# A depthwise convolution's running sum moved from SBUF into one PSUM bank, in strips of eight rows

## The chip, the cores and the metric

The kernel runs on one core of one Trainium2 chip. The metric is the device time of one execution in microseconds (us). A core has five engines that work side by side and meet at semaphores: TensorE (PE in the profile) for matmuls, VectorE (DVE), ScalarE (ACT), GpSimd (POOL) and SyncE (SP), which here only issues DMAs. SBUF is the working memory. PSUM is a smaller memory of eight banks of 512 float32 values per partition; TensorE writes its results there, and VectorE and ScalarE can read and write it.

## The reference, cut to what matters

The input x is 32 images of 56 x 56 pixels and 96 channels, float32. Two residual blocks follow each other: an outlook attention (values, logits from 2 x 2 means, softmax over nine neighbours, sum over overlapping windows, output projection), then a 3 x 3 convolution of each channel by itself. `_gn` is a group norm over three channels and all pixels of an image.

```
    x = x + _L0_conv_ref(_gn(x), L0_conv_W_v, L0_conv_W_a, L0_conv_b_a, L0_conv_W_o, L0_conv_b_o)
    x = x + _L1_conv_ref(_gn(x), L1_conv_w)
    return x
```

The second line is what the change touches. `_L1_conv_ref` clips its nine weights per channel and takes their sign, so the convolution is nine shifted copies of the normed image, each times a number per channel, added up.

## The kernel before, in words

Channels lie on 96 partitions and pixels along the free dimension. One pass of the loop, here called a body, handles one image in a fixed order written out by hand. It has 64 slots (`BODY`), numbered g, 32 for the upper and 32 for the lower half of the image (h is 0 or 1). In every slot TensorE spreads attention weights over channels into a PSUM tile `bc` (`broadcast`, L733), VectorE multiplies it by the values `VAL` into `prod` (`product`, L600), GpSimd adds the two halves of `prod` in 45 of the 64 slots (`pre_add`, L363), and TensorE multiplies by the output weights three slots later and accumulates in `acc` (`add_up`, L753). VectorE adds finished classes of pixels to `X1` (`add_class`, L611). `bc` has two buffers and `prod` four, so TensorE can run up to two slots ahead of VectorE.

Everything else is hung into these slots by the table `AT`: each engine runs through the slots in order and in each does what the table gives it. Entries of 64 and more belong to the next body's pass. The work of three images overlaps: the body of number i multiplies for image i, prepares image i+1 (transposes `IN`, group norm, logits `LOG`, values `V`, softmax), and convolves image i-1.

- Softmax: VectorE takes maxima, sums and inverses (L623, L627, L631); GpSimd subtracts, multiplies and forms the low part of a split number (`SUB` L345, `MUL` L351, `LOW` L356); ScalarE takes exponentials (`EXP` L464), scales the inverse (`UP` L467, in slot 42, which waits for the inverses of slot 43's VectorE work) and writes the high part (`HIGH` L475).
- The uses of the `side` banks: 44 times per body TensorE fills a PSUM bank (`fill_use`: value matmuls L692, logits L698, input transposes L704, output transposes L710, group-norm sums L721) and ScalarE reads it out (`read_use`: L426, L433, L440, L446, L451). The two banks `side[0]` and `side[1]` alternate: the fill of use n waits for the read of use n-2. Input transposes stand in slots 5, 7, 7, 8, 9, 10, 10; the first nine logits in 19 to 23 with up to three in one slot; output transposes in 55 to 60; values in 27 to 33 and 62 to 67. The first read of the values of a half waits until VectorE's last product of that half is done, since it overwrites `VAL`.
- The convolution: ScalarE copies `X1` to `ACC` (L498, slot 1) and, after the norm (`square_1` L506, then GpSimd's small steps L370 to L381), writes the normed image with a rim into `XP` (`rimmed` L527, slot 10). `centre_tap` (L534) starts the sum: ACC = a * ACC + b, in three parts of 19, 19 and 18 rows, in slots 12, 14 and 15. Then VectorE does 24 taps (`tap`, L647), eight taps times three parts: `scalar_tensor_tensor` reads the shifted rows of `XP`, multiplies by the sign, adds `ACC` and writes `ACC`. Both tensors lie in SBUF. They stand in slots 14 to 53. The output transposes wait for all of them.

Two shorter bodies run before the loop (no convolution yet) and one after it (convolution only).

Of the kernel before, what the change touches and what calls it, by code (L numbers as in the profile page):

```python
# [5 lines left out]
BATCH, SIDE, CH = 32, 56, 96  # L6
# [51 lines left out]

    V: ((27, 30, 33, 33), (62, 63, 65, 67)),
    LOG: ((19, 19, 21, 21, 21, 22, 22, 23, 23), (39, 39, 42, 43, 48, 48, 48, 51, 53)),  # L60
# [23 lines left out]
    "rimmed": 10,  # L84
    "centred": (12, 14, 15),
    "taps": (14, 17, 18, 18, 19, 20, 20, 21, 25, 29, 30, 31, 32, 34, 35, 45, 48, 48, 48, 50, 50, 52, 53, 53),
}
PRE = [g for g in range(BODY)
       if TERMS[2 * (g % SLOTS)][0] == TERMS[2 * (g % SLOTS) + 1][0] and g not in AT["not pre"]]
CUTS = (0, 19, 38, SIDE)  # L90
TAP_N = 3 * (KK - 1)
assert len(AT["taps"]) == TAP_N


def pieces(*kinds):
# [20 lines left out]
def upto(per_body, i, n):  # L116

    return (i + 1) * per_body + n


def build_program(nc, x, W_v, W_a, b_a, W_o, b_o, w_conv, ident, group, select, out):
# [3 lines left out]
    with ctx:  # L125
# [287 lines left out]
        def _(act):  # L413
            act.wait_ge(weights_in, 16 * N_W)

            def read_use(i, n, late, kind, which, k):
                bank = side[n % 2]
                until(act, side_full, upto(len(USES), i, n + 1))
                if kind == V:
                    h = which  # L420
                    r0, r1 = V_CUTS[h][k], V_CUTS[h][k + 1]
                    if k == 0:

                        until(act, prod_ready, upto(BODY, i - late, BODY if h else SLOTS))
                    top_row = 1 - h
                    ins = nc.scalar.activation(  # L426
                        VAL[h][:, top_row + r0:top_row + r1, 1:1 + SIDE],
                        bank[0:CH, 0:(r1 - r0) * SIDE].rearrange("c (r w) -> c r w", w=SIDE), ACT.Identity)
                elif kind == LOG:
                    h, cols = which, ROWS[which] * WIN  # L430

                    until(act, fine_step, done(FINE, i - 1, LOW, h, k))
                    ins = nc.scalar.activation(att[h][:, k, :], bank[0:QN, 0:cols],  # L433
                                               ACT.Identity, bias=ba[:, k:k + 1])
                elif kind == IN:
                    if k == 0:

                        until(act, x1_init, upto(1, i, 1))
                        until(act, pool_step, upto(4, i, 0))
                    ins = nc.scalar.activation(X0t[:, 4 * k:4 * k + 4, :],  # L440
                                               bank[0:CH, 0:4 * TP].rearrange("c (t p) -> c t p", t=4), ACT.Identity,
                                               accum_out=sums[:, 0, k:k + 1])
                elif kind == OUT:

                    act.wait_ge(y_out[k % 2], store_no(i, k))
                    ins = nc.scalar.activation(tok_out[:, k % 2, :, :],  # L446
                                               bank[0:TP, 0:4 * CH].rearrange("p (t c) -> p t c", t=4), ACT.Identity)
                else:
                    g = which
                    n_in = chunks(kind, g)  # L450
                    ins = nc.scalar.activation(spill[:, 0:n_in], bank[0:CH, 0:n_in], ACT.Identity,  # L451
                                               accum_out=(nmean if kind == GA else gvar)[:, g:g + 1])
                ins.then_inc(side_read, 1)
# [113 lines left out]
        def _(dve):  # L567
# [66 lines left out]
            def tap(i, n):  # L634
                t, part = divmod(n, 3)
                t += t >= KK // 2
                ty, tx = divmod(t, TAPS)
                r0, r1 = CUTS[part], CUTS[part + 1]
# [39 lines left out]
        def _(pe):  # L678
# [3 lines left out]
            def fill_use(i, n, late, kind, which, k):  # L682
                bank = side[n % 2]

                until(pe, side_read, upto(len(USES), i, n - 1))
                if kind == V:
                    h = which
                    r0, r1 = V_CUTS[h][k], V_CUTS[h][k + 1]
                    if k == 0:

                        until(pe, xn_ready, upto(2, i - late, h + 1))
                    last = nc.tensor.matmul(bank[0:CH, 0:(r1 - r0) * SIDE], wv[:, :], XN[:, r0:r1, :],  # L692
                                            start=True, stop=True)
                elif kind == LOG:
                    h = which
                    if k == 0:
                        until(pe, pool_normed, upto(2, i, h + 1))
                    last = nc.tensor.matmul(bank[0:QN, 0:ROWS[h] * WIN], wa[:, k, :, :],  # L698
                                            pooled[:, 0:ROWS[h], :], start=True, stop=True)
                elif kind == IN:  # L700
                    if k == 0:
                        until(pe, x_in, 16 * (i + 2))
                    for t in range(4):
                        last = nc.tensor.transpose(bank[0:CH, t * TP:(t + 1) * TP], tok_in[:, 4 * k + t, :], idn[:, :])  # L704
                elif kind == OUT:
# [3 lines left out]
                    for t in range(4):  # L709
                        last = nc.tensor.transpose(bank[0:TP, t * CH:(t + 1) * CH], ACCt[:, 4 * k + t, :],  # L710
                                                   idn[0:CH, 0:CH])
                else:
# [98 lines left out]
```

## Time and profile before

| | |
|---|---|
| three timed runs | 5112.86, 5118.91 (median), 5120.16 us |
| span of the profiled execution | 5120.9 us, 0.04% above that median |
| its time outside the span | the page gives none; the span is used as its own time |
| VectorE busy | 4730.3 us, 92% |
| TensorE busy | 4119.3 us, 80% |
| GpSimd busy | 4037.2 us, 79% |
| ScalarE busy | 2005.6 us, 39% |
| granted TensorE clock, mean | 0.850 of full |

An engine's busy time counts what it executes, also when an instruction is being held up inside; waiting for a semaphore is idle time. A clock of 1.00 is 2.4 GHz and 0.50 is 1.2 GHz; windows in between mix the two levels. Where timelines print "x3", three instructions of one kind are merged into one line with their time from first start to last end.

### The profile page before, as it was taken

How to read it: one execution, taken by the hardware profiler on the slowest of the kernel's cores; microseconds unless marked ns; L12 is line 12 of the kernel's file. 1: busy time of each engine (PE TensorE's matmuls, PEld its weight loads, DVE VectorE, ACT ScalarE, POOL GpSimd, SP SyncE). 2: the span in 40 equal slices, each digit the busy share in tenths (PEclk: the TensorE clock that was granted, in tenths of full speed). 3: DMA queues.
4: the chain of work that ended last, by engine and by line, in shares of the span. 5: the costliest groups of instructions: out<-in, count | busy, mean ns of one | idle time of the engine just before them, and what ended most of it. 6: DMA issues, size and time to landing. Idle time of an engine off the chain costs nothing.

```text
span 5120.9 us, 55367 instructions
## 1 busy us (share of the span) xinstructions
PE 4119.3 (80%) x13632; PEld 2114.1 (41%) x13632; DVE 4730.3 (92%) x3723; ACT 2005.6 (39%) x2753; POOL 4037.2 (79%) x3628
## 2 busy tenths in 40 slices
PE   4877887878887888878788887888878888878885
PEld 2434444434444344444344443444434444434442
DVE  5799999999999999999999999999999999999997
ACT  4424444334443344432444433444324444334431
POOL 5787877877877888778878788787787787887883
PEclk7988888888888788888888888888888888888887
DMA  1110111101111111111011111111110111111111
GB/s 39 38 38 24 47 44 37 47 21 40 47 33 47 36 25 47 42 39 47 21 40 47 33 47 30 31 47 38 43 47 15 46 47 33 47 24 37 47 29 28
DMA packets 126083, 194.36 MB, mean 38 GB/s; under 512 B 14248, under 2 KB 115464, under 8 KB 122472
## 3 DMA queue, kind: packets, MB, share of 16 engines
q1 hardware_dynamic: 97384, 155.50, 13.0%
q10 hardware_dynamic: 28672, 38.55, 2.5%
q8 instruction: 11, 0.18, 0.0%
q14 instruction: 16, 0.13, 0.0%
HBM read 39.22 MB, written 38.54 MB: 15 GB/s over the span
## 4 chain that ended last, share of the span: by engine, by line
POOL 45%; issue 25%; PE 18%; ACT 5%; DVE 5%; DMA 1%; SPq 0%; DVEq 0%; POOLq 0%; ACTq 0%; PEldq 0%; PEld 0%
POOL prod L363 15%; POOL part L356 10%; POOL att L351 10%; PE acc L753 10%; POOL att L345 6%; PE bc L733 4%; DVE prod L600 2%; ACT X L440 2%; POOL pc L332 2%; PE side L698 2%; ACT X L523 2%; PE side L692 1%; DVE ACC L647 1%; PE side L710 1%; DVE top L631 1%
## 5 line engine op out<-in xcount | busy, mean ns | idle before, releaser
L753 PE MATMUL acc<-prod,wo 96*96 96x392 f32 x5312 | 2478.5, 573 | 161.8 <-POOL prod L363 155.7
L600 DVE TENSOR_TENSOR prod<-bc,VAL 96x784 f32<-96x784 f32 x2048 | 1928.2, 959 | 307.5 <-PE bc L733 289.4
L363 POOL TENSOR_TENSOR prod<-prod 96x392 f32<-96x392 f32 x1440 | 1685.5, 1178 | 501.3 <-DVE prod L600 491.7
L733 PE MATMUL bc<-stack,sel 96*96 96x392 f16 x4608 | 1303.2, 378 | 633.5 <-DVE prod L600 611.5
L647 DVE SCALAR_TENSOR_TENSOR ACC<-XP,sg,ACC 96x1064 f32<-96x1064 f32 (+1 forms) x768 | 1736.2, 2281 | 14.9 <-ACT ACC L534 13.8
L753 PEld LDWEIGHTS acc<-prod,wo 96*96 96x96 f32 x5312 | 982.1, 188 | 675.1 <-issue 271.6
L733 PEld LDWEIGHTS bc<-stack,sel 96*96 96x96 f16 x4608 | 576.2, 137 | 1571.4 <-DVE prod L600 972.2
L351 POOL TENSOR_TENSOR att<-att,top 108x420 f32<-108x420 f32 (+1 forms) x576 | 750.3, 1321 | 38.3 <-ACT top L467 38.3
L345 POOL TENSOR_TENSOR att<-att,top 108x420 f32<-108x420 f32 (+1 forms) x576 | 645.1, 1138 | 144.2 <-DVE top L623 144.2
L356 POOL TENSOR_TENSOR part<-att,part 108x420 f16<-108x420 f32 (+1 forms) x576 | 737.3, 1298 | 0.0
L433 ACT ACTIVATE att<-side,ba 108x420 f32<-108x420 f32 (+1 forms) x576 | 340.5, 597 | 671.6 <-PE side L698 659.0
L698 PE MATMUL side<-pooled,wa 96*108 96x392 f32 (+1 forms) x1152 | 528.0, 573 | 46.3 <-ACT att L433 23.2
L627 DVE TENSOR_REDUCE top<-att 108x105 f32<-108x945 f32 (+1 forms) x256 | 456.9, 1796 | 14.5 <-ACT att L464 14.5
L623 DVE TENSOR_REDUCE top<-att 108x105 f32<-108x945 f32 (+1 forms) x256 | 449.3, 1786 | 15.4 <-ACTq L247 13.2
L426 ACT ACTIVATE VAL<-side 96x392 f32<-96x392 f32 (+1 forms) x256 | 124.7, 512 | 857.5 <-DVE prod L600 713.5
L475 ACT ACTIVATE part<-att 108x1260 f16<-108x1260 f32 (+1 forms) x192 | 234.5, 1221 | 470.4 <-POOL att L351 470.2
L698 PEld LDWEIGHTS side<-pooled,wa 96*108 96x108 f32 x1152 | 221.6, 197 | 305.4 <-issue 224.0
L446 ACT ACTIVATE tok_out<-side 112x384 f32<-112x384 f32 x224 | 110.2, 492 | 605.7 <-PE side L710 304.6
L464 ACT ACTIVATE att<-att 108x1260 f32<-108x1260 f32 (+1 forms) x192 | 232.4, 1210 | 140.5 <-POOL att L345 140.5
L692 PE MATMUL side<-XN,wv 96*96 96x392 f32 (+1 forms) x512 | 244.1, 573 | 7.8 <-ACT tok_out L446 3.8
L370 POOL TENSOR_TENSOR gve<-eps,gvar 96x1 f32<-96x1 f32 x64 | 13.2, 206 | 281.8 <-ACT spill L451 268.8
L440 ACT ACTIVATE X<-side 96x448 f32<-96x448 f32 x224 | 204.2, 1000 | 29.4 <-PE side L704 28.2
(55 smaller groups left out, 2183.7 us busy)
## 6 DMA issues: line engine op xcount, KB each, us to landing
stack<-part SPq DMA_DIRECT2D x192, 275.3 KB
stack<-part SPq DMA_DIRECT2D x192, 256.9 KB
tok_in<-in_x SPq DMA_DIRECT2D x32, 1176.0 KB, 9.7
out<-tok_out ACTq DMA_DIRECT2D x224, 168.0 KB, 4.2
stack<-part SPq DMA_DIRECT2D x192, 30.5 KB
stack<-part SPq DMA_DIRECT2D x192, 28.5 KB
X<-in_L_conv_W_a SPq DMA_DIRECT2D x1, 364.5 KB
ACC<-select SPq DMA_DIRECT2D x1, 144.0 KB
```

The costliest lines, as they stand in the source:

```text
L345: nc.gpsimd.tensor_tensor(att[h][:, k, :], att[h][:, k, :], top[h][:, :], ALU.subtract).then_inc(fine_step, 1)
L351: nc.gpsimd.tensor_tensor(att[h][:, k, :], att[h][:, k, :], top[h][:, :], ALU.mult).then_inc(fine_step, 1)
L356: nc.gpsimd.tensor_tensor(low, a4(h)[:, k], high, ALU.subtract).then_inc(fine_step, 1)
L363: nc.gpsimd.tensor_tensor(p[:, 0, :], p[:, 0, :], p[:, 1, :], ALU.add).then_inc(pre_added, 1)
L433: ins = nc.scalar.activation(att[h][:, k, :], bank[0:QN, 0:cols], ACT.Identity, bias=ba[:, k:k + 1])
L600: nc.vector.tensor_tensor(prod[:, g % PRODUCTS, :, :].rearrange("c a (i j) -> c a i j", j=WIN), b, v, ALU.mult).then_inc(prod_ready, 1)
L623: ins = nc.vector.tensor_reduce(top[h][:, c], by_window[:, c, :], AX.X, ALU.max)
L627: ins = nc.vector.tensor_reduce(top[h][:, c], by_window[:, c, :], AX.X, ALU.add)
L647: nc.vector.scalar_tensor_tensor(a, XP[:, r0 + ty:r1 + ty, tx:tx + SIDE], sg[:, t:t + 1], a, ALU.mult, ALU.add).then_inc(tapped, 1)
L698: last = nc.tensor.matmul(bank[0:QN, 0:ROWS[h] * WIN], wa[:, k, :, :], pooled[:, 0:ROWS[h], :], start=True, stop=True)
L733: last = nc.tensor.matmul(bc[g % 2][0:CH, a, 0:UNIT], sel[:, which, :], stack[h][:, qi, ki * TAPS + kj, si:si + HALF, sj:sj + WIN], start= ...
L753: last = nc.tensor.matmul(acc[c % 2][0:CH, 0:UNIT], wo[:, :], prod[:, g % PRODUCTS, a, :], start=first, stop=s == LAST[c] and (g in PRE or ...
```

## The change

`ACC` is no longer updated tap by tap. The image is cut into seven strips of eight rows (448 values). ScalarE's `centre_tap` writes a strip's start into a PSUM bank `strip`, VectorE adds seven taps there, reading and writing PSUM, and the eighth tap writes the strip's result to `ACC` in SBUF. Only one bank holds strips, so the start of strip s+1 waits for the last tap of strip s. The order of loops turns over: all taps of a strip, then the next strip, so taps are now 56 small ones in a chain instead of 24 large ones in three. The bank comes from the `side` pair, which becomes a single bank: the fill of use n waits for the read of use n-1. The second value fill moves from slot 30 to slot 31.

```diff
-    V: ((27, 30, 33, 33), (62, 63, 65, 67)),
+    V: ((27, 31, 33, 33), (62, 63, 65, 67)),
...
-    "centred": (12, 14, 15),
-    "taps": (14, 17, 18, 18, 19, 20, 20, 21, 25, 29, 30, 31, 32, 34, 35, 45, 48, 48, 48, 50, 50, 52, 53, 53),
+    "centred": (12, 18, 24, 30, 36, 42, 48),
+    "taps": (13, 13, 14, 15, 15, 16, 17, 17, 19, 19, 20, 21, 21, 22, 23, 23, 25, 25, 26, 27, 27, 28, 29, 29, 31, 31, 32, 33, 33, 34, 35, 35, 37, 37, 38, 39, 39, 40, 41, 41, 43, 43, 44, 45, 45, 46, 47, 47, 49, 49, 50, 51, 51, 52, 53, 53),
...
-CUTS = (0, 19, 38, SIDE)
-TAP_N = 3 * (KK - 1)
+STRIP = 8
+STRIPS = SIDE // STRIP
+TAP_N = STRIPS * (KK - 1)
...
-        side = [ctx.enter_context(nc.psum_tensor(f"side{b}", [128, 512], F32)) for b in range(2)]
+        strip = ctx.enter_context(nc.psum_tensor("strip", [128, 512], F32))
+        side = ctx.enter_context(nc.psum_tensor("side", [128, 512], F32))
...
+        stripv = strip[0:CH, 0:STRIP * SIDE].rearrange("c (r w) -> c r w", w=SIDE)
...
-                a = ACC[:, CUTS[part]:CUTS[part + 1], :]
-                nc.scalar.activation(a, a, ACT.Identity, bias=centre[:, 2:3], scale=centre[:, 1:2]).then_inc(centred, 1)
+                until(act, tapped, upto(TAP_N, i, (KK - 1) * part))
+                nc.scalar.activation(stripv, ACC[:, STRIP * part:STRIP * (part + 1), :], ACT.Identity,
+                                     bias=centre[:, 2:3], scale=centre[:, 1:2]).then_inc(centred, 1)
...
-                t, part = divmod(n, 3)
+                part, t = divmod(n, KK - 1)
+                last = t == KK - 2
                 t += t >= KK // 2
...
-                if n < 3:
-                    until(dve, centred, upto(3, i, n + 1))
+                if n % (KK - 1) == 0:
+                    until(dve, centred, upto(STRIPS, i, part + 1))
                 else:
-                    until(dve, tapped, upto(TAP_N, i, n - 2))
-                a = ACC[:, r0:r1, :]
-                nc.vector.scalar_tensor_tensor(a, XP[:, r0 + ty:r1 + ty, tx:tx + SIDE], sg[:, t:t + 1], a,
+                    until(dve, tapped, upto(TAP_N, i, n))
+                nc.vector.scalar_tensor_tensor(ACC[:, r0:r1, :] if last else stripv,
+                                               XP[:, r0 + ty:r1 + ty, tx:tx + SIDE], sg[:, t:t + 1], stripv,
                                                ALU.mult, ALU.add).then_inc(tapped, 1)
...
-                until(pe, side_read, upto(len(USES), i, n - 1))
+                until(pe, side_read, upto(len(USES), i, n))
```

All other lines of the diff replace `bank` (that is `side[n % 2]`) by `side`, without another effect.

## Rows read from the trace of the kernel before

**Rows 1.** The page's first part: busy time of each engine, its share, instructions.

```profile
PE 4119.3 (80%) x13632; PEld 2114.1 (41%) x13632; DVE 4730.3 (92%) x3723; ACT 2005.6 (39%) x2753; POOL 4037.2 (79%) x3628
```

**Rows 2.** The page's groups: busy us, mean ns, idle us before, releaser.

```profile
L600 DVE TENSOR_TENSOR prod<-bc,VAL 96x784 f32<-96x784 f32 x2048 | 1928.2, 959 | 307.5 <-PE bc L733 289.4
...
L647 DVE SCALAR_TENSOR_TENSOR ACC<-XP,sg,ACC 96x1064 f32<-96x1064 f32 (+1 forms) x768 | 1736.2, 2281 | 14.9 <-ACT ACC L534 13.8
```

**Rows 3.** Single lines: duration in ns as minimum/median/maximum, first and last start.

```profile
L647 DVE SCALAR_TENSOR_TENSOR ACC<-XP,sg,ACC x768: 1247/2004/6940, 257.4 to 5107.4; 96x1064 f32<-96x1064 f32 x128, 96x1008 f32<-96x1008 f32 x64
...
L363 POOL TENSOR_TENSOR prod<-prod x1440: 998/1016/2104, 101.3 to 5061.3; 96x392 f32<-96x392 f32 x180
...
L611 DVE TENSOR_TENSOR X<-acc,X x256: 546/551/565, 129.9 to 5063.6; 96x392 f32<-96x392 f32 x128
```

**Rows 4.** VectorE's timeline, taps of slots 14, 45 and 48: start us, us.

```profile
2609.10 5.98 DVE L647 SCALAR_TENSOR_TENSOR ACC<-XP,sg,ACC 96x1064 f32<-96x1064 f32 x1
...
2690.78 1.32 DVE L647 SCALAR_TENSOR_TENSOR ACC<-XP,sg,ACC 96x1064 f32<-96x1064 f32 x1
...
2695.32 10.85 DVE L647 SCALAR_TENSOR_TENSOR ACC<-XP,sg,ACC 96x1064 f32<-96x1064 f32 x3
```

**Rows 5.** TensorE's timeline behind those three taps.

```profile
2699.63 0.82 PE L753 MATMUL acc<-prod,wo 96*96 96x392 f32 x2
2707.12 0.89 PE L733 MATMUL bc<-stack,sel 96*96 96x392 f16 x2 [6.67 <-DVE prod L600]
2707.80 1.51 PE L753 MATMUL acc<-prod,wo 96*96 96x392 f32 x2
```

**Rows 6.** The window after: length; busy of PE, PEld, DVE, ACT, POOL; granted clock; DMA.

```profile
2707.00:2720.80 13.80, 13.14 (x28) 6.22 (x29) 13.80 (x12) 2.43 (x3) 13.66 (x10) 0.54 0.29 68
```

**Rows 7.** ScalarE's timeline, slots 4 to 10.

```profile
2591.27 2.90 ACT L523 ACTIVATE X<-X,bo 96x3136 f32<-96x3136 f32 x1
...
2594.34 1.01 ACT L440 ACTIVATE X<-side 96x448 f32<-96x448 f32 x1
...
2595.20 1.00 ACT L440 ACTIVATE X<-side 96x448 f32<-96x448 f32 x1
...
2603.96 3.01 ACT L527 ACTIVATE XP<-ACC,shift,rstd 96x3136 f32<-96x3136 f32 x1
```

**Rows 8.** TensorE's timeline, input transposes of slots 5 and 7.

```profile
2590.67 0.57 PE L704 MATMUL side<-idn,tok_in 112*96 112x112 f32 x4
...
2594.37 0.59 PE L704 MATMUL side<-idn,tok_in 112*96 112x112 f32 x4
2595.41 0.59 PE L704 MATMUL side<-idn,tok_in 112*96 112x112 f32 x4 [0.45 <-ACT X L440]
```

**Rows 9.** TensorE's two logit fills of slot 22.

```profile
2632.44 1.57 PE L698 MATMUL side<-pooled,wa 96*108 96x420 f32 x4
```

**Rows 10.** The end of a body on VectorE: slot 63, then slots 0 and 1.

```profile
2738.53 0.97 DVE L600 TENSOR_TENSOR prod<-bc,VAL 96x784 f32<-96x784 f32 x1 [2.21 <-PE bc L733]
...
2740.28 1.97 DVE L600 TENSOR_TENSOR prod<-bc,VAL 96x784 f32<-96x784 f32 x2 [0.31 <-PE bc L733]
```

**Rows 11.** ScalarE's first value reads behind the product of slot 63.

```profile
2739.54 0.93 ACT L426 ACTIVATE VAL<-side 96x448 f32<-96x448 f32 x2 [2.64 <-DVE prod L600]
```

**Rows 12.** Groups by form: ScalarE's logit reads, `UP`, centre taps.

```profile
L433 ACT ACTIVATE att<-side,ba 108x420 f32<-108x420 f32 x288 | 175.7, 610 | 178.2 <-PE side L698 166.8
...
L534 ACT ACTIVATE ACC<-ACC,centre 96x1064 f32<-96x1064 f32 x64 | 81.0, 1266 | 0.8 <-issue 0.6 <-ACT XP L527 0.2
...
L467 ACT ACTIVATE top<-top 108x420 f32<-108x420 f32 x32 | 17.8, 556 | 67.1 <-DVE top L631 67.1
```

**Rows 13.** `start_acc`, once per body from body 1 to 32: minimum/median/maximum, starts.

```profile
L498 ACT ACTIVATE ACC<-X x32: 2802/2820/2825, 235.3 to 5064.2; 96x3136 f32<-96x3136 f32 x32
```

**Rows 14.** VectorE's timeline of the last body: seven taps in a row.

```profile
5079.31 8.63 DVE L647 SCALAR_TENSOR_TENSOR ACC<-XP,sg,ACC 96x1064 f32<-96x1064 f32 x7 [0.19 <-ACT ACC L534]
```

**Rows 15.** Waits in the whole execution: who for whom, us, times, longest.

```profile
ACT tok_out L446 <- DMA out<-tok_out: 294.0, 130, 5.9
```

More of the change, by code:

```diff
@@ L427, in read_use @@
                         VAL[h][:, top_row + r0:top_row + r1, 1:1 + SIDE],
-                        bank[0:CH, 0:(r1 - r0) * SIDE].rearrange("c (r w) -> c r w", w=SIDE), ACT.Identity)
+                        side[0:CH, 0:(r1 - r0) * SIDE].rearrange("c (r w) -> c r w", w=SIDE), ACT.Identity)
                 elif kind == LOG:
@@ L432, in read_use @@
                     until(act, fine_step, done(FINE, i - 1, LOW, h, k))
-                    ins = nc.scalar.activation(att[h][:, k, :], bank[0:QN, 0:cols],
+                    ins = nc.scalar.activation(att[h][:, k, :], side[0:QN, 0:cols],
                                                ACT.Identity, bias=ba[:, k:k + 1])
@@ L440, in read_use @@
                     ins = nc.scalar.activation(X0t[:, 4 * k:4 * k + 4, :],
-                                               bank[0:CH, 0:4 * TP].rearrange("c (t p) -> c t p", t=4), ACT.Identity,
+                                               side[0:CH, 0:4 * TP].rearrange("c (t p) -> c t p", t=4), ACT.Identity,
                                                accum_out=sums[:, 0, k:k + 1])
@@ L446, in read_use @@
                     ins = nc.scalar.activation(tok_out[:, k % 2, :, :],
-                                               bank[0:TP, 0:4 * CH].rearrange("p (t c) -> p t c", t=4), ACT.Identity)
+                                               side[0:TP, 0:4 * CH].rearrange("p (t c) -> p t c", t=4), ACT.Identity)
                 else:
@@ L450, in read_use @@
                     n_in = chunks(kind, g)
-                    ins = nc.scalar.activation(spill[:, 0:n_in], bank[0:CH, 0:n_in], ACT.Identity,
+                    ins = nc.scalar.activation(spill[:, 0:n_in], side[0:CH, 0:n_in], ACT.Identity,
                                                accum_out=(nmean if kind == GA else gvar)[:, g:g + 1])
@@ L691, in fill_use @@
                         until(pe, xn_ready, upto(2, i - late, h + 1))
-                    last = nc.tensor.matmul(bank[0:CH, 0:(r1 - r0) * SIDE], wv[:, :], XN[:, r0:r1, :],
+                    last = nc.tensor.matmul(side[0:CH, 0:(r1 - r0) * SIDE], wv[:, :], XN[:, r0:r1, :],
                                             start=True, stop=True)
@@ L697, in fill_use @@
                         until(pe, pool_normed, upto(2, i, h + 1))
-                    last = nc.tensor.matmul(bank[0:QN, 0:ROWS[h] * WIN], wa[:, k, :, :],
+                    last = nc.tensor.matmul(side[0:QN, 0:ROWS[h] * WIN], wa[:, k, :, :],
                                             pooled[:, 0:ROWS[h], :], start=True, stop=True)
@@ L703, in fill_use @@
                     for t in range(4):
-                        last = nc.tensor.transpose(bank[0:CH, t * TP:(t + 1) * TP], tok_in[:, 4 * k + t, :], idn[:, :])
+                        last = nc.tensor.transpose(side[0:CH, t * TP:(t + 1) * TP], tok_in[:, 4 * k + t, :], idn[:, :])
                 elif kind == OUT:
@@ L709, in fill_use @@
                     for t in range(4):
-                        last = nc.tensor.transpose(bank[0:TP, t * CH:(t + 1) * CH], ACCt[:, 4 * k + t, :],
+                        last = nc.tensor.transpose(side[0:TP, t * CH:(t + 1) * CH], ACCt[:, 4 * k + t, :],
                                                    idn[0:CH, 0:CH])
@@ L720, in fill_use @@
                     src = (sums if kind == GA else squares)[:, g, 0:chunks(kind, g)]
-                    last = nc.tensor.matmul(bank[0:CH, 0:chunks(kind, g)], grp[:, :], src, start=True, stop=True)
+                    last = nc.tensor.matmul(side[0:CH, 0:chunks(kind, g)], grp[:, :], src, start=True, stop=True)
                 last.then_inc(side_full, 1)
```

5 lines of the change are left out of this document (1 added, 4 removed).

## The prediction, made before the changed kernel ran

> **What bounds the kernel now.** I read the engine totals first [rows 1]: VectorE is busy 92% of the span, TensorE 80%, GpSimd 79%. Then the groups by form and the single lines [rows 2, 3]. The taps stand out twice. Their mean is 2281 ns, but the shortest takes 1247 ns and the longest 6940. The products (784 values, one operand in PSUM) lie at 959 ns. GpSimd's pre-adds lie mostly at 1016 ns, but reach 2104. So taps are stretched, and so is GpSimd beside them. VectorE's timeline shows it: the tap of slot 45 takes 1.32 us, the three of slot 48 take 10.85 [rows 4]. TensorE stands for 6.67 us behind these three, and its next projection pair takes 1.51 us where the one before took 0.82 [rows 5]: granted 0.54 in the window from there, with TensorE busy 13.14 of 13.80 us [rows 6]. VectorE waits for `bc` only 289 us in all [rows 2]. It is the bound, and some of what bounds it is taps held up inside. One body lasts (5064.2 - 235.3)/31 = 155.8 us [rows 13].
>
> **Taps.** Before: 24 x 2.281 = 54.7 us per body [rows 2]. Seven taps in a row take 8.63 us [rows 14], a step of 1.23 against 1.31 each, so overlap hides 0.08 per instruction: 54.7 - 24 x 0.08 = 52.8 us. After: 56 taps of 448 values. No row shows VectorE writing PSUM. Products and class adds give 784 values in 959 ns and 392 in 551, a slope of 1.04 ns per value and 143 ns fixed; 448 values make 0.61 us. The fixed part of a free tap is 1247 - 1008 x 1.04 = about 200 ns [rows 3], which makes 0.67. Far above, if reading and writing the bank shared a cycle, lies 2 x 0.467 + 0.2 = 1.13; far below I know nothing that would beat 0.47, one value per 1.04 ns with nothing fixed. I take 0.64, between the two nearest rows, a step of 0.56. 21 of the taps stand directly behind the tap that they depend on and lose the overlap, 0.08 each. After: 56 x 0.56 + 21 x 0.08 = 33.1 us. **Gain 19.7 us per body.** Of it some 23 us is the hold-up that goes (24 x (2.28 - 1.3)); smaller instructions give 4 back. GpSimd's stretched instructions get short too, which is worth nothing by itself while VectorE sets the pace.
>
> The Trainium skill (VectorE: DVE Perf Modes, the section on the TRN2 errata) has a rule against this: a VectorE instruction that reads PSUM pays 120 fixed cycles, one that reads SBUF 58. By it, at the page's 0.96 GHz, 56 taps on PSUM would pay an estimated 56 x 62 cycles = 3.6 us more per body than as many on SBUF. The rows here show the reverse, about 140 ns with a PSUM operand and 200 for the SBUF tap [rows 3]. The measurement decides.
>
> **What the single side bank adds.** VectorE's stalls, in the order of slots, for a body:
> - *Slots 5 to 10.* Input reads follow each other at 0.86 us (2594.34 to 2595.20) because the next bank is already filled [rows 7]. Now each fill waits for the read: 1.01 + 0.59 + two handoffs of some 0.06 (a fill begins at 2595.41, that read ends at 2595.35 [rows 7, 8]) = 1.7. The first fill now comes only after `start_x1` (ends 2594.17), not at 2590.67; TensorE holds slots 6 and 7 behind it, and they take 2594.37 - 2590.67 = 3.7 us less the fill [rows 7, 8]. Added up: the first read comes 0.7 late; the second another 2.8 (reads 0.86 apart before, now 1.0 + 3.1 of slots 6 and 7 with the fill, less what ran beside the read); the third, fifth, sixth and seventh 0.8 each. So `rimmed` starts some 6.8 us later than its 2603.96, at 2610.8, ends 3.0 later, and with `UP` (0.5) and a strip start (0.6 to 0.7) the first tap comes at 2615.0 where it came at 2609.10 [rows 4, 7]. That is 5.9, and since it stands one slot earlier VectorE has a product less (0.88) ahead of it. **+6.7 us.** ScalarE works there with no gap, so nothing hides it. Queued behind it are the `bc` of slots 6 to 13.
> - *Slots 19 to 23.* Two logit fills take 1.57 us [rows 9], their read 0.61 [rows 12]. Five of nine fills now wait for a read in the same slot, 0.61 + 2 x 0.06 each: 3.6. With nine fills (6.5) and five slots of `bc` and projection (1.0 each, at the speed of [rows 5]' first row) TensorE needs 15.1 us. VectorE needs only 10 now (five products, eight taps, a class add). **+5 us.** Logits in 39 to 53 are spread more and stay under the maxima and sums.
> - *Slot 31.* ScalarE stands in slot 27 until product 31 is done; the strip start of slot 30 is queued behind that read. The tap waits 0.54 + 0.72 + handoffs = **+1.3**. 0.72 is an estimate between 610 ns for 420 values read from PSUM and 1266 for 1064 from SBUF, nearer to the second's kind [rows 12].
> - *Slot 43.* `UP` stands before the strip start on ScalarE and waits for slot 43's inverse, and the tap waits behind both: 0.56 [rows 12] + 0.72 = **+1.3**.
> - *Slot 63.* Product 63 ends at 2739.50, products 0 and 1 start at 2740.28 [rows 10]; ScalarE reads two filled banks from 2739.54 [rows 11]. Now it reads one, TensorE fills the next (0.75) and only then spreads slot 0: **+1.3**.
> - *Slots 55 to 60.* ScalarE waits 294 us in all for stores [rows 15], and TensorE now feels it one fill sooner: **+0.7**; there is slack of a store or two.
> - Short waits of 1.7 us in slots 18 to 34 go under in these.
>
> Sum: -19.7 + 6.7 + 5 + 1.3 + 1.3 + 1.3 + 0.7 - 1.7 = **-5.1 us**, times 31 = -158.
>
> **The ends.** The last body has only the convolution: before 24 taps at a step of 1.23 and a few waits, some 31 us, after 56 x 0.67 in a chain plus seven strip starts of 0.84 = 43.4, less 0.5 for a shorter first start: +12. The two bodies before the loop have no taps to gain from and pay the handoffs: 14 transposes and the logits, an estimate of +19 from the 0.84 and 0.72 above. Sum: 5120.9 - 158 + 31 = 4994, against a median of 5118.9 with a span 0.04% above it. I forecast 4995 us.
>
> **Rivals.**
> 1. *The handoffs are hidden.* TensorE makes up for the waits, as it can be two slots ahead, and GpSimd's and the clock's gains help. For it: TensorE is busy 4119.3/32 = 129 us of a body, and that at a clock of 0.85. Against it: ScalarE has no gap from 2591 to 2604 [rows 7]. Time: 5120.9 - 19.7 x 31 + 31 = 4541; with half the handoffs 4770. Chance 0.16.
> 2. *Slower: TensorE's clock falls in slots 4 to 13.* TensorE now stands about 3 us before the first input fill and 2.5 us behind `square_1`. After 6.67 us of standing it ran projections at 1.51 instead of 0.82 per pair [rows 5]; if that comes here, six slots (6, 7, 10 to 13) with some 1.5 us of work each cost 9 us more, since `bc` is what VectorE waits for there. -5.1 + 9 = +3.9: 5121 + 121 + 31 = 5273. It decides from 4.1 us per body on. Against it: the new waits are less than half as long as the 6.67, and the long stalls behind held-up taps go, which gives clock back. Chance 0.17.
> 3. *The taps stay dear.* PSUM read and write share a cycle (1.13 us each, 27 us more per body, 5830), or GpSimd still holds up a tap with one SBUF operand (5650). Against the second: class adds have one such operand and never leave 546 to 565 ns, whatever GpSimd does [rows 3]. Chance 0.04.
> 4. *Nothing measurable*: the stalls are 4 to 5 us dearer and eat all. Chance 0.06.
>
> The Trainium skill (TensorE: Matmul & The Clock Gate, on what is actually happening) says of rival 2 that "the default state is throttled, and activity releases the throttle"; [rows 5] agree. By that rule shorter waits behind the taps help and new ones hurt. The Trainium skill (SBUF — State Buffer, on who interferes with whom) speaks for the gain: a VectorE instruction with at most one SBUF input does not contend with GpSimd; the steady class adds agree [rows 3].
>
> **How the numbers follow.** The forecast case has 0.57. Its own range is 4890 to 5110: the tap between 0.61 and 0.67 makes 1.7 us per body, 52 in all, and the stalls in slots 5 to 10 and 19 to 23 are good to 2 us. The whole range, 4790 to 5240, takes half of rival 1 and most of rival 2. A difference under 0.2% can't be told from none. Faster 0.72: the forecast case but for 0.03 and rival 1, and a little of rival 2 with a short clock loss; same 0.07; slower 0.21.
>
> **What would show it.** Right: taps at 0.61 to 0.67 us with a maximum near their median, pre-adds never above 1.1 us, VectorE's share near 80%, its wait for `bc` grown from 289 us to some 600 or more, most in slots 5 to 23. Wrong: taps above 0.8 us (the sum is void), `rimmed` not later against slot 0 (rival 1), granted clock at 0.5 in slots 5 to 13 (rival 2).

## The result and the profile after

| | before | after |
|---|---|---|
| median of the timed runs | 5117.11 us (5112.86 to 5120.16) | 5480.64 us (5455.98 to 5488.69) |
| ratio to before, 95% interval | | 1.0705 [1.0681, 1.073] |
| span of the profiled execution | 5120.9 us | 5486.9 us |
| granted TensorE clock, mean | 0.850 | 0.856 |

The kernel became 7% slower; forecast was 2.4% faster. The totals of the kernel after, to be held against [rows 1]:

```profile
PE 4230.9 (77%) x13632; PEld 2134.1 (39%) x13632; DVE 4199.3 (77%) x4747; ACT 2066.6 (38%) x2881; POOL 3359.8 (61%) x3628
```

VectorE's work fell by 531 us, 16.6 for each of 32 bodies, where the forecast counted 19.7. Its idle time rose from 391 to 1288 us. The groups of the kernel after (busy us, mean ns, idle us before, what ended most of that idle time, called the releaser):

```profile
L603 DVE TENSOR_TENSOR prod<-bc,VAL 96x784 f32<-96x784 f32 x2048 | 1965.4, 966 | 1047.1 <-PE bc L736 978.1
...
L650 DVE SCALAR_TENSOR_TENSOR strip<-XP,sg,strip 96x448 f32<-96x448 f32 x1568 | 1063.2, 678 | 121.3 <-ACT strip L536 102.9
```

and its single lines (minimum/median/maximum in ns, first and last start):

```profile
L650 DVE SCALAR_TENSOR_TENSOR strip<-XP,sg,strip x1568: 601/676/703, 298.3 to 5472.5; 96x448 f32<-96x448 f32 x196
...
L366 POOL TENSOR_TENSOR prod<-prod x1440: 997/1013/1058, 120.9 to 5412.1; 96x392 f32<-96x392 f32 x180
...
L500 ACT ACTIVATE ACC<-X x32: 2816/2817/2820, 266.9 to 5415.0; 96x3136 f32<-96x3136 f32 x32
```

No tap is held up any more: the maximum is 703 ns, where [rows 3] had 6940 (the 224 eighth taps, which write `ACC`, never take over 680), and no pre-add takes more than 1058 ns (2104 before). But VectorE's wait for `bc` grew from 289 to 978 us. A body lasts (5415.0 - 266.9)/31 = 166.1 us, 10.3 more than before. The front grew by 266.9 - 235.3 = 31.6 and the tail from 56.7 to 71.9, by 15.2. Sum: 31 x 10.3 + 46.8 = 366, the difference of the spans.

The list of waits of the kernel after shows the single bank directly (who for whom: us, times, longest us). PEld is TensorE's loading of weights, which overlaps its matmuls, so the two kinds of lines do not add up.

```profile
PEld side L701 <- ACT att L435: 484.5, 357, 3.8
...
PE side L701 <- ACT att L435: 234.1, 264, 2.6
...
PEld side L707 <- ACT X L442: 199.9, 129, 2.8
...
PE side L707 <- ACT X L442: 135.9, 97, 2.1
...
PE side L707 <- ACT spill L453: 121.3, 60, 3.7
```

The same waits of TensorE's matmuls before, where the 0.45 of [rows 8] is one of the first line's:

```profile
PE side L704 <- ACT X L440: 26.8, 62, 0.5
PE side L698 <- ACT att L433: 23.2, 32, 2.8
```

**Slots 5 to 10.** ScalarE's timeline of one body, then TensorE's and VectorE's:

```profile
2621.80 2.89 ACT L525 ACTIVATE X<-X,bo 96x3136 f32<-96x3136 f32 x1
...
2626.07 0.98 ACT L442 ACTIVATE X<-side 96x448 f32<-96x448 f32 x1 [1.23 <-PE side L707]
...
2631.44 1.00 ACT L442 ACTIVATE X<-side 96x448 f32<-96x448 f32 x1 [4.39 <-PE side L707]
2632.23 0.21 ACT L442 ACTIVATION_READ_ACCUMULATOR X<-side 96x1 f32 x1
2633.13 1.01 ACT L442 ACTIVATE X<-side 96x448 f32<-96x448 f32 x1 [0.68 <-PE side L707]
...
2644.25 3.00 ACT L529 ACTIVATE XP<-ACC,shift,rstd 96x3136 f32<-96x3136 f32 x1
```

```profile
2624.97 0.98 PE L707 MATMUL side<-idn,tok_in 112*96 112x112 f32 x4 [3.69 <-ACT spill L453]
2625.74 1.51 PE L736 MATMUL bc<-stack,sel 96*96 96x392 f16 x4
2627.05 2.79 PE L756 MATMUL acc<-prod,wo 96*96 96x392 f32 x4
```

```profile
2627.29 0.97 DVE L603 TENSOR_TENSOR prod<-bc,VAL 96x784 f32<-96x784 f32 x1 [6.08 <-PE bc L736]
```

`start_x1` (2621.80) holds the spill read behind it, the spill read holds TensorE for 3.69 us, VectorE stands 6.08. Behind this TensorE's four projection matmuls take 2.79 us, 0.70 each, where the pair in [rows 5]' first row took 0.41 each. From `start_x1` to `rimmed` it is 2644.25 - 2621.80 = 22.45 us, before 12.69 [rows 7]: 9.8 more. The windows of slots 0 to 13 and 13 to 24 (columns as in [rows 6]) show the clock: 0.81 in the first, 1.00 in the second.

```profile
2613.20:2649.70 36.50, 27.81 (x105) 15.59 (x103) 22.90 (x22) 23.66 (x31) 16.22 (x21) 0.81 0.00 0
2649.70:2676.40 26.70, 21.87 (x78) 10.65 (x77) 20.17 (x30) 15.47 (x23) 20.58 (x25) 1.00 0.01 4
```

**Slot 48.** It has three logit fills in a row. On TensorE and then VectorE:

```profile
2574.56 1.08 PE L701 MATMUL side<-pooled,wa 96*108 96x392 f32 x2
2576.40 0.91 PE L701 MATMUL side<-pooled,wa 96*108 96x392 f32 x2 [0.76 <-ACT att L435]
2578.07 1.26 PE L701 MATMUL side<-pooled,wa 96*108 96x392 f32 x2 [0.76 <-ACT att L435]
2579.12 0.86 PE L736 MATMUL bc<-stack,sel 96*96 96x392 f16 x2
```

```profile
2580.01 0.97 DVE L603 TENSOR_TENSOR prod<-bc,VAL 96x784 f32<-96x784 f32 x1 [5.07 <-PE bc L736]
```

The prediction had put these logits at nothing.

A table by slot, worked out from the starts of the 2048 products, mean over bodies 2 to 29, in us. A column goes from the product of its first slot to that of its second, the last one to product 0 of the next body. The experiments in it are told below:

```
slots     period  0-5  5-13 13-19 19-24 24-31 31-36 36-43 43-48 48-54 54-59 59-63 63-0
before     156.9  7.2  17.8  18.8  12.3  17.6  15.0  14.8   7.1  25.9  11.7   6.8  1.9
after      167.5  7.0  28.5  10.9  16.9  19.0  12.1  20.8  12.5  17.0  11.5   8.0  3.2
e1         174.4  7.2  29.0  17.9  15.4  17.2  15.1  17.3   7.1  25.9  11.9   7.4  3.0
e3         172.3  6.4  18.2  17.8  16.0  21.6  15.2  21.3  14.6  18.9  11.6   7.3  3.5
e2c        155.8  8.1  17.6  18.5  11.9  17.6  14.7  15.5   7.4  23.2  12.9   6.4  2.0
e2         146.7  7.4  17.5  10.4  11.3  18.9  11.3  21.2  12.4  13.9  11.1   7.6  3.7
d1         155.0  7.2  17.6  10.4  18.3  18.8  11.4  21.0  12.3  15.6  11.1   7.7  3.4
d2         156.6  7.3  27.2  10.4  11.3  19.0  11.3  21.3  12.4  14.0  11.1   7.7  3.5
d3         150.0  8.0  18.5  10.4  11.3  18.9  11.7  21.2  12.5  14.3  11.3   8.4  3.4
c2         154.1  8.8  18.3  11.4  11.2  19.8  12.1  21.5  13.3  15.0  12.7   6.1  3.8
f1         169.0  7.0  27.5  10.9  19.7  18.9  11.9  20.8  12.6  17.0  11.5   8.0  3.3
g1         174.5  7.0  29.7  10.9  19.9  18.9  12.0  21.4  12.2  15.2  12.8  11.2  3.2
k1         143.4  9.7  17.5   9.2  12.3  17.6  10.0  20.2  11.0  12.9  12.1   5.7  5.2
```

Where taps had been held up (slots 13 to 19, 48 to 54) the change wins 16.8 us; slots 5 to 13 lose 10.7, slots 19 to 24 lose 4.6; slots 36 to 48 lose 11.4, mainly because they hold 16 of the new taps and had one (with two side banks, in e2, they lose 11.7).

### The profile page after: what moved, and what is told of

Same layout as the page of the kernel before. It is cut to its first block, busy times and chain, and to the rows that moved or that the text cites. A ratio compares the mean times of both kernels' runs of the same rounds, so it can differ in the third digit from the quotient of the medians.

```text
span 5486.9 us, 57919 instructions
## 1 busy us (share of the span) xinstructions
PE 4230.9 (77%) x13632; PEld 2134.1 (39%) x13632; DVE 4199.3 (77%) x4747; ACT 2066.6 (38%) x2881; POOL 3359.8 (61%) x3628
## 4 chain that ended last, share of the span: by engine, by line
PE 42%; DVE 24%; issue 19%; ACT 10%; POOL 2%; DVEq 1%; ACTq 1%; SPq 0%; DMA 0%; POOLq 0%; PEldq 0%; PEld 0%
PE acc L756 20%; PE bc L736 10%; DVE strip L650 7%; DVE prod L603 7%; PE side L701 6%; DVE top L626 4%; DVE top L630 3%; PE side L695 3%; PE side L707 3%; ACT att L435 2%; DVE top L634 2%; ACT X L525 2%; ACT X L442 1%; ACT att L466 1%; PE side L713 1%
## 5 line engine op out<-in xcount | busy, mean ns | idle before, releaser
L603 DVE TENSOR_TENSOR prod<-bc,VAL 96x784 f32<-96x784 f32 x2048 | 1965.4, 966 | 1047.1 <-PE bc L736 978.1
L366 POOL TENSOR_TENSOR prod<-prod 96x392 f32<-96x392 f32 x1440 | 1452.9, 1015 | 1430.9 <-DVE prod L603 1424.1
L756 PEld LDWEIGHTS acc<-prod,wo 96*96 96x96 f32 x5312 | 1003.0, 189 | 499.0 <-issue 292.2
L650 DVE SCALAR_TENSOR_TENSOR strip<-XP,sg,strip 96x448 f32<-96x448 f32 x1568 | 1063.2, 678 | 121.3 <-ACT strip L536 102.9
L701 PE MATMUL side<-pooled,wa 96*108 96x392 f32 (+1 forms) x1152 | 593.2, 601 | 248.1 <-ACT att L435 234.1
L348 POOL TENSOR_TENSOR att<-att,top 108x420 f32<-108x420 f32 (+1 forms) x576 | 591.3, 1044 | 176.1 <-DVE top L626 176.1
L354 POOL TENSOR_TENSOR att<-att,top 108x420 f32<-108x420 f32 (+1 forms) x576 | 591.2, 1046 | 38.3 <-ACT top L469 38.3
L359 POOL TENSOR_TENSOR part<-att,part 108x420 f16<-108x420 f32 (+1 forms) x576 | 523.6, 928 | 0.0
L701 PEld LDWEIGHTS side<-pooled,wa 96*108 96x108 f32 x1152 | 196.2, 196 | 596.1 <-ACT att L435 484.5
L707 PE MATMUL side<-idn,tok_in 112*96 112x112 f32 x896 | 168.4, 325 | 279.5 <-ACT X L442 135.9
L707 PEld LDWEIGHTS side<-idn,tok_in 112*96 112x96 f32 x896 | 107.6, 153 | 358.3 <-ACT X L442 199.9
## 6 DMA issues: line engine op xcount, KB each, us to landing
stack<-part SPq DMA_DIRECT2D x192, 28.5 KB
```

Of the source, the lines that this page charges most:

```text
L348: nc.gpsimd.tensor_tensor(att[h][:, k, :], att[h][:, k, :], top[h][:, :], ALU.subtract).then_inc(fine_step, 1)
L354: nc.gpsimd.tensor_tensor(att[h][:, k, :], att[h][:, k, :], top[h][:, :], ALU.mult).then_inc(fine_step, 1)
L359: nc.gpsimd.tensor_tensor(low, a4(h)[:, k], high, ALU.subtract).then_inc(fine_step, 1)
L366: nc.gpsimd.tensor_tensor(p[:, 0, :], p[:, 0, :], p[:, 1, :], ALU.add).then_inc(pre_added, 1)
L603: nc.vector.tensor_tensor(prod[:, g % PRODUCTS, :, :].rearrange("c a (i j) -> c a i j", j=WIN), b, v, ALU.mult).then_inc(prod_ready, 1)
L650: nc.vector.scalar_tensor_tensor(ACC[:, r0:r1, :] if last else stripv, XP[:, r0 + ty:r1 + ty, tx:tx + SIDE], sg[:, t:t + 1], stripv, ALU.m ...
```

## The experiments

Three theories stood after the result. S: the single side bank costs more than the 12.0 us per body that the prediction gives it (6.7 + 5 + 1.3 for slot 63 + 0.7 - 1.7; the 1.3 of slot 31 and of slot 43 come from the strip starts). V: what VectorE saves is refilled by its waits for `bc`. C: the clock fall in slots 5 to 13 is much of it. All times are medians, ratios are to the kernel before. The kernel before ran again with each group of experiments, with medians from 5117 to 5125 us, so a difference between runs of two groups is good to some 10 us.

### The two halves apart

**e1**, the kernel before with a single side bank and the second value fill in slot 31:

```diff
-    V: ((27, 30, 33, 33), (62, 63, 65, 67)),
+    V: ((27, 31, 33, 33), (62, 63, 65, 67)),
...
-                until(pe, side_read, upto(len(USES), i, n - 1))
+                until(pe, side_read, upto(len(USES), i, n))
```

> The kernel before with one side bank and the value fill of slot 30 in slot 31; taps unchanged in SBUF. Theory A (the hand-over fill-read-fill on one side bank is what costs; I sized it too small): VectorE still has its long taps, so part of the handoffs hides under them; I expect 5117 + 31 x 12 to 20 us = 5490 to 5740, with GpSimd's pre-adds still up to 2.1 us. Theory B (the loss comes from the chained strips and small taps, the single bank is nearly free): within 1% of 5117, below 5170.

Measured: 5671.82 us, 1.1074 [1.1052, 1.1095]. The kernel before took 5125.22 us beside it: the bank alone costs 547 us, 17.5 per body by the table. That is theory A, and more than the 12.0 of the prediction.

**e2**, the kernel after with two side banks (its edit is shown against the kernel after). To free a bank `acc` is single, and the four classes of a half are accumulated as one; 6 of 8 class adds of a body are left out.

```diff
-                until(pe, side_read, upto(len(USES), i, n))
+                until(pe, side_read, upto(len(USES), i, n - 1))
...
-                    first = t == 0 or TERMS[t - 1][0] != c
+                    first = t == 0
...
-                        until(pe, y_added, upto(8, i, 4 * h + c - 1))
+                        until(pe, y_added, upto(2, i, h))
```

> The changed kernel with two side banks again; the bank comes from acc, which is single here because the four pixel classes of a half are accumulated in one group and only the last of eight class adds is done (six adds of 0.55 us per body are left out, so it does not add those classes apart). To be read against its control e2c. Theory A: the tap gain of about 18 us per body appears: 540 to 620 us faster than e2c, some 4480 to 4600. Theory B: chained strips cost as much as they gain: within 100 us of e2c.

Measured: 4841.35 us, 0.9452 [0.9436, 0.9467]. It lies between the two theories, which had up to some 4600 and from some 4990.

**e2c**, the control: the kernel before with the same merged classes.

> The kernel before with the same simplification as e2 (one acc bank, one class group and add per half, six adds of 0.55 us per body left out). Both theories: 5117 less up to 6 x 0.48 x 31 = 90 us of VectorE work: 5010 to 5110.

Measured: 5093.29 us, 0.9938 [0.9918, 0.9957]. Its totals:

```profile
PE 4137.4 (81%) x13632; PEld 2106.2 (41%) x13632; DVE 4465.1 (88%) x3531; ACT 2010.5 (39%) x2753; POOL 4064.4 (80%) x3628
```

VectorE works 265 us less than before, by the missing adds and because taps are held up less, and only 24 us of it show (32 against the 5125.22 measured beside it): a first sign for V. I count e2's omission at those 24; what it is worth in a kernel with strips was not measured by itself. The strips with two banks bring 5093 - 4841 = 252 us, half of what the prediction counts (19.7 x 31 = 611, less 12 in the tail). Going back to one bank costs 5481 - 4841 - 24 = 615 us, if the omission is worth the same there. In the table e2c to e2 is -9.1 per body and e2 to after +20.8, of which 1.1 is the classes': the bank costs 19.7. e1, without that omission, has 17.5. S holds.

**e3**, strips and their order as after, but the running sum in SBUF as before, two side banks, two `acc` banks (shown against the kernel after; eight classes and all adds as before):

```diff
-                nc.vector.scalar_tensor_tensor(ACC[:, r0:r1, :] if last else stripv,
-                                               XP[:, r0 + ty:r1 + ty, tx:tx + SIDE], sg[:, t:t + 1], stripv,
+                a = ACC[:, r0:r1, :]
+                nc.vector.scalar_tensor_tensor(a, XP[:, r0 + ty:r1 + ty, tx:tx + SIDE], sg[:, t:t + 1], a,
...
```

> The kernel before (two side banks) with the strip order: seven strip starts and 56 chained taps of 448 values, all in SBUF. It tells the strip order from the PSUM operand. Theory A: taps are still held up by GpSimd (some from 0.68 up to several us), the chained order by itself costs 32 more instructions of 0.2 us and a few waits on the strip start: 5117 + 31 x 6 to 14 = 5300 to 5550. Rival: with small taps GpSimd gets in between, the hold-ups shrink and it is as fast as before or faster, below 5120.

Measured: 5613.33 us, 1.0959 [1.0939, 1.098], 63 us above theory A's range and far from the rival. Its taps in the list of lines, then in the groups:

```profile
L649 DVE SCALAR_TENSOR_TENSOR ACC<-XP,sg,ACC x1792: 579/681/6400, 262.2 to 5598.0; 96x448 f32<-96x448 f32 x200
```

```profile
L649 DVE SCALAR_TENSOR_TENSOR ACC<-XP,sg,ACC 96x448 f32<-96x448 f32 x1792 | 1967.3, 1098 | 161.7 <-ACT ACC L536 135.5 <-DVE ACC L649 0.2 <-issue 0.2
```

A free small tap in SBUF is as fast as one in PSUM (median 681 against 676 ns); the worst takes nine times the median. With the classes' 24 us allowed for, the change is a sum of three, taken in this order: strips and their order +496, their place in PSUM 4841 + 24 - 5613 = -748, the single bank +615, together +363.

### Which hand-over costs what

**d1, d2, d3**: e2, with the wait of a single bank for some uses only: logits in d1; input transposes and sums in d2; values and output transposes in d3.

```diff
-                until(pe, side_read, upto(len(USES), i, n - 1))
+                until(pe, side_read, upto(len(USES), i, n if kind in (LOG,) else n - 1))
```

> e2 (strips in PSUM, two side banks, class groups merged; 4841 us), with one wait more: each logit fill waits for the read of the use before it, as on a single bank. It leaves out what e2 leaves out. Theory A1 (the sizes of the prediction hold, the logits of slots 19 to 23 cost 5 us per body and those of 39 to 53 nothing): 4841 + 31 x 5 = 5000. Theory A2 (the lower half's logits cost as well, above all the three of slot 48, and the clock falls behind them): 31 x 9 to 13, 5120 to 5240.

> e2 with the hand-over wait for the input transposes and the group-norm sums alone. Theory A1: +6.7 us per body: 5050. Theory A2 (TensorE's clock falls in the new waits of slots 5 to 11 and makes bc late): +9 to 12 us per body: 5120 to 5210.

> e2 with the hand-over wait for the value matmuls and the output transposes alone. Theory A1: +1.3 and +0.7 us per body, 4900. A rival: the output transposes wait for stores through it and delay the values behind them: +5 or more per body, above 5000. If d1, d2 and d3 add up to far less than 615 us (the step from e2's gain to the changed kernel), the waits hurt only together.

Measured: 5096.13 us, 0.995 [0.9933, 0.9967]; 5137.24, 1.0024 [1.0013, 1.0035]; 4931.09, 0.9605 [0.9571, 0.9638]. Above e2 that is 255, 296 and 90 us, per body 8.3, 9.9 and 3.3 in the table; in all 641. That is close to the 615 of all together, so they roughly add up. All three lie above the prediction's own sizes (theories A1: 5000, 5050 and 4900): d2 in the range of A2, d1 just below it, d3 by 31 us. The logits cost 7.0 in slots 19 to 24 and 1.7 in 48 to 54; the inputs 9.7 in slots 5 to 13.

### Is it the clock?

Granted clock in slots 5 to 13, worked out from the records over bodies 2 to 29: before 0.94, e2 0.91, after 0.76, e1 0.74, d2 0.77. The other way round, slots 59 to 63 are at 0.67 before and 0.58 after. **f1**, the kernel after with four useless matmuls of 448 columns in slot 5, ahead of the group-norm sum, so that TensorE works while `start_x1` runs:

```diff
+                        for _ in range(4):
+                            nc.tensor.matmul(side[0:CH, 0:448], wv[:, :], XN[:, 0:8, :], start=True, stop=True)
```

> The changed kernel with useless work added: four value matmuls of 448 columns (about 3 us) into the free side bank in slot 5, before the group-norm sum, where TensorE stands 3.7 us. Theory K (the clock that falls in that wait makes slots 5 to 7 about 3 us longer): granted clock 1.00 from slot 5 on, 2 to 4 us less per body, 5360 to 5420. Theory W (the wait itself is the cost): unchanged or up to 1% slower, 5480 to 5530.

Measured: 5532.1 us, 1.0794 [1.0776, 1.0812], 0.9% slower than the kernel after, as theory W said. TensorE's timeline has them (eight instructions), what is left of the stall (0.76 us of 3.69), and then the four projection matmuls behind it:

```profile
2641.82 3.25 PE L721 MATMUL side<-XN,wv 96*96 96x448 f32 x8
...
2645.91 0.58 PE L707 MATMUL side<-idn,tok_in 112*96 112x112 f32 x4 [0.76 <-ACT spill L453]
...
2647.03 1.48 PE L758 MATMUL acc<-prod,wo 96*96 96x392 f32 x4
```

The four now take 1.48 us, 0.37 each, instead of 2.79: behind the stall the clock is up. Slots 5 to 13 get 1.0 us shorter (28.5 to 27.5), with 0.81 over the whole stretch. But slots 19 to 24 grow from 16.9 to 19.7, at 0.83 instead of 0.98. So in f1 the clock was mended in one place and there was no gain in sum.

The traces bound what slower matmuls can be of the bank's cost. In slots 5 to 13 TensorE is busy 15.7 us before and 19.9 after, and idle 2.1 and 8.7: of the 10.7 us that these slots grow, about 4.2 are longer work at a lower clock and 6.6 are standing. From e2 to d2 it is 4.0 of 9.7 (busy 15.7 to 19.7). In the totals TensorE's busy time grows from e2 to after by 4230.9 - 3971.7 = 259 us, of 639 us between their times; from before to e1 by 328, of 547. These are upper estimates, since longer work counts only where it is waited for. So C is not the main cause in the kernel after, but it may be up to two fifths of what the bank costs there, and more in e1:

```profile
PE 4447.5 (78%) x13632; PEld 2210.8 (39%) x13632; DVE 4717.2 (83%) x3723; ACT 2031.7 (36%) x2753; POOL 4039.6 (71%) x3628
```

**g1**, the kernel after with the lower half's logits one to a slot:

```diff
-    LOG: ((19, 19, 21, 21, 21, 22, 22, 23, 23), (39, 39, 42, 43, 48, 48, 48, 51, 53)),
+    LOG: ((19, 19, 21, 21, 21, 22, 22, 23, 23), (39, 41, 42, 44, 46, 48, 50, 52, 53)),
```

> The changed kernel with the nine logits of the lower half in slots 39, 41, 42, 44, 46, 48, 50, 52, 53, no two in one slot, instead of 39, 39, 42, 43, 48, 48, 48, 51, 53. Theory S (fills in the same slot are what costs): the 5 us stall at slot 49 goes, 3 to 6 us less per body, 5300 to 5390. Theory T (every hand-over costs, spread or not): within 40 us of 5481.

Measured: 5678.27 us, 1.1076 [1.1057, 1.1094]: 198 us slower than after, against what I expected. Slots 48 to 54 do win 1.8 us, but 54 to 63 lose 4.5 and 19 to 24 lose 3.0, at a clock of 0.83 there. Its wait list has

```profile
DVE prod L603 <- PE bc L736: 1139.9, 796, 6.1
```

What puts the loss into other slots was not isolated.

### How much of VectorE's work counts

**h1** and **k1**: taps only on the upper four of a strip's eight rows (half of the convolution is left out), on the kernel after and on e2:

```diff
+                m = r0 + STRIP // 2
-                nc.vector.scalar_tensor_tensor(ACC[:, r0:r1, :] if last else stripv,
+                nc.vector.scalar_tensor_tensor(ACC[:, r0:m, :] if last else stripv[:, 0:STRIP // 2, :],
...
```

> The changed kernel with taps of half the size: 224 values instead of 448, so half of each strip's rows is left out. Taps take 0.44 instead of 0.68 us: 56 x 0.23 = 13 us less VectorE work per body. Theory P (VectorE no longer sets the pace of the changed kernel): less than half of it shows, under 6 us per body, above 5290. Rival (it still does): 5481 - 13 x 31 = 5080.

> e2 (strips in PSUM, two side banks, merged class groups; 4841 us) with taps of 224 values, half of each strip left out: 13 us less VectorE work per body. Theory V (with two banks VectorE still sets the pace, and e2's small gain has another cause): 4841 - 13 x 31 = 4440 to 4500. Theory T (the strips freed more of VectorE than TensorE can follow): no more than half shows, 4640 to 4800.

Measured: h1 5202.59 us, 1.0145 [1.012, 1.017]; k1 4704.9, 0.9185 [0.917, 0.9201]. Totals of h1, then of e2 and of k1:

```profile
PE 4137.0 (79%) x13632; PEld 2097.9 (40%) x13632; DVE 3793.6 (73%) x4747; ACT 2057.9 (39%) x2881; POOL 3359.3 (64%) x3628
```

```profile
PE 3971.7 (82%) x13632; PEld 2072.4 (43%) x13632; DVE 4086.3 (85%) x4555; ACT 2037.7 (42%) x2881; POOL 3359.2 (69%) x3628
```

```profile
PE 3933.1 (84%) x13632; PEld 2056.6 (44%) x13632; DVE 3684.9 (78%) x4555; ACT 2039.8 (43%) x2881; POOL 3351.1 (71%) x3628
```

VectorE works 406 us less in h1 and 401 in k1; the time falls by 278 and by 136 us. Two thirds and one third show: h1 lies between its two theories, k1 is theory T. In k1 3.8 us per body are lost again between slot 63 and slot 5, and the granted clock of slots 0 to 5 is 0.69 (e2: 0.98); how much of the missing two thirds that is was not isolated. **k2** takes work from TensorE instead: e2 without the second projection of the 19 slots that have two (their half of `prod` is left out of the output), 1216 matmul instructions less.

```diff
-                for a in range(1 if g in PRE else 2):
+                for a in range(1):
```

> e2 with the second projection of the 19 slots per body that have two left out: 19 x 0.66 = 12.5 us less TensorE work per body at full clock. Theory T: it shows in full or more, since the handoff to bc gets shorter, 4400 to 4550. Theory V: under a third of it, above 4720.

Measured: 4731.31 us, 0.9248 [0.9232, 0.9263]. Totals, then the waits of k2 and of e2 for `bc`:

```profile
PE 3682.9 (78%) x12416; PEld 1872.0 (40%) x12416; DVE 4075.8 (86%) x4555; ACT 2025.1 (43%) x2881; POOL 3353.3 (71%) x3628
...
DVE prod L604 <- PE bc L736: 325.1, 300, 4.3
```

```profile
DVE prod L604 <- PE bc L736: 421.9, 395, 4.3
```

TensorE works 289 us less, and 110 show (the time lies in the range of the expectation's theory V, though 110 are 38% of the 289). Relief of either engine shows in part: e2 is bounded by neither alone, but by the two in turn, through `bc` and `prod`. V holds, with that addition. In which slots which of them leads was not measured, nor whether GpSimd (69% in e2) or ScalarE (42%) adds a limit.

### A better place to take the bank from

44 fills per body pass through `side`, 8 class changes through `acc`. **c2** is the whole kernel with strips in PSUM, two side banks and a single `acc`. VectorE empties it as soon as a class is full; classes 0 and 2 end on the first of a slot's two projections, so that one signals.

```diff
-            add_at = {min(LAST[c] + LAG + 1, SLOTS - 1): c for c in range(3)}
+            add_at = {14: 0, 22: 1, 29: 2}
...
-                        until(pe, y_added, upto(8, i, 4 * h + c - 1))
+                        until(pe, y_added, upto(8, i, 4 * h + c))
...
+                    if a == 0 and TERMS[t + 1][0] != c:
+                        last.then_inc(class_full, 1)
```

> A complete kernel: the changed kernel with two side banks, the bank taken from acc, which is single. All eight class adds are done; the adds of classes 0, 1, 2 move to slots 14, 22, 29 of each half, and a new class waits for the add of the one before. Theory A (44 uses per body make a single side bank dear, eight class changes make a single acc bank cheap): e2's 4841 plus six adds (90 us) plus eight handoffs of up to 1 us: 4930 to 5100, faster than both. Rival: TensorE loses its lead at each class change and it costs 1.5 us or more each: 5250 or more, slower than the kernel before.

Measured: 5061.32 us (5037.91 to 5065.06), 0.9863 [0.9838, 0.9889]: faster than both kernels, by 1.4% than the one before, and 220 us above e2, whose omitted adds it does and whose single `acc` it must empty eight times. Its new waits, then its wait for `bc`:

```profile
PEld acc L762 <- DVE X L619: 351.9, 218, 2.3
...
PE acc L762 <- DVE X L619: 204.8, 223, 2.0
...
DVE prod L605 <- PE bc L742: 510.6, 507, 4.4
```

**c3**: on c2, with strip starts first in their slot, the first value fill in slot 31 instead of 27, and two exponentials in slots 34 and 35 instead of 36 and 37.

> c2 (complete, two side banks, one acc bank; 5061 us) with the strip starts put ahead of the other ScalarE work of their slot, the exponentials in slots 33, 34, 35 and the first value fill in slot 31 instead of 27. Theory A: the three waits on strip starts and on the exponential in slots 31, 36 and 43 (1.1 to 1.2 us each in c2's trace) go: 5061 - 31 x 3.4 = 4955. Rival: TensorE and its clock set the pace there and the waits turn into waits for bc: 5030 to 5070.

Measured: 5047.6 us (5027.83 to 5061.16), 0.984 [0.9819, 0.986]. It overlaps with c2, so the retouching is not shown to gain, and theory A's 4955 did not come.

```profile
DVE prod L605 <- PE bc L742: 589.5, 485, 4.1
```

## Why the prediction was wrong, by its steps

- **The hold-up goes: right.** 703 ns at most, pre-adds at 1058, as was said, and e3 shows it is the place in PSUM and not the size or order of taps. The Trainium skill (SBUF — State Buffer, on who interferes with whom) says that a VectorE instruction with two SBUF inputs contends with a GpSimd instruction that reads SBUF, and one with at most one SBUF input, outside the modes that use two ports, does not; e3's 6400 ns and after's 703 agree.
- **The tap: slightly low.** 0.678 us where 0.64 stood, 56 x 0.038 = 2.1 us per body (the prediction's two neighbours were 0.61 and 0.67); the free tap of [rows 3] with its 200 ns, 0.67, was the right neighbour. Rival 3 did not come, nor did rivals 1 and 4.
- **"Gain 19.7 us per body": the work saved was nearly right (16.6), but it does not show in full.** This is the first step that failed. The prediction called VectorE the bound and let all that it saves count, less new stalls. For the strips alone it had -19.7 + 1.3 + 1.3 = -17.1; e2 against e2c has -9.1. h1 and k1 show two thirds and one third of a saving. TensorE was at 80% [rows 1], at most two slots ahead and released by VectorE's own products, so it was the next limit at once; k2, which relieves TensorE alone and is 110 us faster than e2, agrees.
- **"What the single side bank adds": mis-sized.** This is the second. 12.0 in the prediction, 19.7 measured (17.5 in e1, where taps are still held up). By group: *slots 5 to 10* +6.7, measured 9.7 (d2) to 10.7; `rimmed` came 9.8 later against `start_x1`, not 6.8. TensorE stands 6.6 us more there, near what was forecast; the term left out that its work gets longer at the lower clock, up to 4.2 us. *Slots 19 to 23* +5, measured 7.0 in d1; nine fills at the 1.57 per two of [rows 9] are 7.1 us, not 6.5. *Strip starts of slots 31 and 43* +2.6: VectorE waits 102.9 us in all for them, 3.2 per body, near it. *Values and output transposes* 1.3 + 0.7, measured 3.3 in d3. *"Logits in 39 to 53 are spread more and stay under the maxima and sums"*: wrong, three of them stand in slot 48 of the table, TensorE stands 0.76 us before the second and the third, VectorE waits 5.07; d1 puts 1.7 us on it.
- **Rival 2, the clock in slots 4 to 13: came in part.** The granted clock there fell from 0.94 to 0.76, and these slots took 10.7 us more instead of 6.7. The longer work of TensorE there, 4.2 us at most, is what the rival can claim, not its 9; and the result lies 208 us above its 5273 all the same.
- **The ends: +31, measured +46.8** (31.6 and 15.2); the tail's +12 was near, the front's +19 too low.
- **The sum.** Forecast -5.1 us per body, in the table +10.6. Of the 15.7 between them 8.0 are gain of the strips that doesn't show (-9.1 for -17.1) and 7.7 are the bank (19.7 for 12.0). The range ended at 5240 because it held the first for certain and the second for good to 2 us.
- **The signs to look for.** VectorE's share: forecast near 80%, is 77. Wait for `bc`: "some 600 or more", is 978, most of it where stalls were foretold and in slots 48 to 54.

## What to carry to other kernels

Before a bank is taken from a pool, count the hand-overs that pass through it per round: here the same bank cost 19.7 us per body out of the pool with 44 and left a net gain out of the one with 8. A saving on the busiest engine counts only up to the next engine that waits for it; where two engines hand buffers to and fro, the runs here showed a tenth of it (e2c, from 92% and 80% busy) to two thirds (h1, from 77% each). Look at every slot in which several fills of one pool stand behind each other, not at the mean spread over the table; but spreading them was no gain here by itself (g1).

## What was not expected of the hardware

- The same chain of small taps costs some 748 us more with the running sum in SBUF than in PSUM (e3 against e2), while an undisturbed one takes the same time (681 and 676 ns).
- The clock mended in one place fell in another: in f1 0.37 us per projection matmul instead of 0.70 behind the stall, then 0.83 instead of 0.98 in slots 19 to 24. g1 has the same 0.83 there, though nothing of those slots was changed. Why is not shown.
- The mean clock is no guide: it rose from 0.850 to 0.856 in a kernel that is 7% slower.
